# A six-layer megakernel on one core: weight loads, statistics and normalizations ahead of its mLSTM layer in another order

## The chip, the cores and the metric

The kernel runs on one core of one Trainium2 chip. One launch computes all six layers. The metric is the device time of the launch in microseconds (us), the median of several runs.

## The reference

The input x has 32 batches of 256 tokens with 128 channels, all float32. Six blocks are added to x one after another: an expert-choice feed-forward ("choice"), an RWKV attention, the first feed-forward again, a top-2 mixture of experts ("top2"), an mLSTM attention, and the top2 mixture again. Each block first normalizes x over its channels, without a gain.

```python
x = x + 0.5 * _L0_ffn_ref(_layernorm(x), ...)        # choice
x = x + _L0_attn_ref(_layernorm(x), ...)             # rwkv
x = x + 0.5 * _L0_ffn_ref(_layernorm(x), ...)        # choice
x = x + 0.5 * _L1_ffn_ref(_layernorm(x), ...)        # top2
x = x + _L1_attn_ref(_layernorm(x), ...)             # mlstm
x = x + 0.5 * _L1_ffn_ref(_layernorm(x), ...)        # top2
# mlstm, NH = 4 heads of DH = 32:
q, k, v, o = x @ Wq, x @ Wk, x @ Wv, x @ Wo
ig = 15 * tanh((x @ Wig + big) / 15); fg = 15 * tanh((x @ Wfg + bfg) / 15)
log_D[i, j] = cumsum(log_sigmoid(fg))[i] - cumsum(...)[j] + ig[j]   for j <= i
m = max_j log_D; D = exp(log_D - m); C = (q @ k.T) / sqrt(DH) * D
h = C @ v / (max(|C.sum(-1)|, exp(-m)) + 1e-6)
out = (sigmoid(o) * multi_head_norm(h)) @ Wdown
```

The gates ig and fg need every token of every batch before the cumulated sums are taken, so in the kernel all 32 batches pass through the gate product before the first step of the attention itself.

## The kernel before, in words

X, the whole activation, lives in SBUF as 64 tiles of 128 tokens by 128 channels; a batch is two tiles. The program is written engine by engine with explicit semaphores, and each engine runs its instructions in the order in which the code writes them. Six layers follow each other; between most of them the work overlaps batch by batch. The first top2 layer is different: its blocks write their rows to a table in DRAM (rt_y) by token number, so X can be loaded back only when all blocks have been sent. This is where the change lies.

At the end of the first top2 layer, SyncE (SP) waits for all sends and then issues eight loads of X, each of a "piece" of FB = 4 batches (`Top2.sync`, L894 to L896). VectorE (DVE), at the end of `Top2.vector` (L827 to L829), waits for each piece, adds 4 to the semaphore x_done and calls `Moments.moments_loaded` (L236): eight bn_stats, one a tile (`spread`, L266), and eight bn_aggr (`gather`, L272). GpSimd (POOL) makes from these the negative mean and the reciprocal deviation of the piece in three instructions on 128 by 8 numbers (`Moments.rstd`, L284, L285, L295) and counts them in the semaphore "scaled". The statistics have two buffers, so a piece's statistics wait until the piece two before has been scaled.

Then the mLSTM layer begins. SP, TensorE (PE), ScalarE (ACT) and DVE wait in `Shared.start` until x_done has counted all 32 batches. SP issues seven loads of weights and biases (`Mlstm.sync`, L1769 to L1771). DVE waits for them (L2105), sets a column of ones, scales Wdown by the head norm's weights (L2106, L2107), and normalizes batch after batch (`Normed.vector`, L332: two instructions, one a tile, into two alternating buffers mlstm_xn; batch b waits until the transposes of batch b-2 have read the buffer). For each batch PE makes two transposes into a PSUM bank (`turn_first`, L1792) and, after ACT has copied them to SBUF as mlstm_xT (L1899), two narrow products with the gate weights (`score`, L1801). When all 32 batches are scored, DVE does the gate math (`gate_math`, from L1989), PE transposes the gates, DVE takes the cumulated sums (`row_math`), and at the end of that chain the attention's steps start. The PE also waits, before its first transpose, for the scaled Wdown.

The same form of work stands once more in the program, at its very start: the first choice layer takes statistics of the loaded pieces and, behind each piece, normalizes the four batches of the piece before (`moments_first` with `between`).

The three lines that name the order in the first layer:

```python
            self.take(dve, FB * c, FB, FB * c, slice(0, FB * TP), c % 2)
            if between is not None and c:
                between(c - 1)
```

Of the kernel before, what the change touches and what calls it, by code (L numbers as in the profile page):

```python
# [24 lines left out]
B, T, C = 32, 256, 128  # L25
TP = T // P
# [16 lines left out]
FB = 4  # L43
# [149 lines left out]
class Moments:  # L193
# [39 lines left out]
        if layer < len(LAYERS) and inside(b):  # L233
            self.rstd(pool, layer, b, 1, b, slice(0, TP), u)

    def moments_loaded(self, dve, layer, c):  # L236
        n = layer * B + FB * c
        if c == 0:
            dve.wait_ge(self.scaled, n)
        self.take(dve, n, FB, FB * c, slice(0, FB * TP), c % 2)  # L240

    def scale_loaded(self, pool, layer, c):
        self.rstd(pool, layer, c, FB, FB * c, slice(0, FB * TP), c % 2)
# [134 lines left out]
class Top2(Layer):  # L378
# [392 lines left out]

    def vector(self, dve):
        sh, w = self.sh, self.w
        m = sh.moments
        for r, part in self.ORDER[2:]:
            (self.choose if part == "choose" else self.page)(dve, r)
        if not self.run:
# [43 lines left out]
        xlo(0, 0)  # L821
        xlo(0, 1)
        self.blocks(dve, step, 0, self.NBLK + 2)

        if self.run:
            return
        for c in range(XC):  # L827
            dve.wait_ge(sh.x_loaded[c], 32).then_inc(sh.x_done, FB)
            m.moments_loaded(dve, self.layer + 1, c)  # L829


    def centring(self, pool):
# [38 lines left out]
    def sync(self, sp):  # L871
        d = self.dispatch
        self.w.split.once(sp, self.w.sync)
        self.w.split.ready(sp)
        sp.wait_ge(self.sent, 16 * NT * (self.run + 1))

        def load(i, u):
            m = u % self.RING
            v, n = self.ring(i, u, -self.RING, self.YR)
            if self.block(i, u, -self.RING) or self.run:  # L880
                need(sp, self.y_sent[v], 16 * n)
            sp.dma_start(self.xs[:, m, :], d.region[self.run][bass.ds(P * (self.RING * i + u), P), :]).then_inc(self.xs_in[m], 16)

        def step(i, u):
            if self.block(i, u):
                load(i, u)

        self.blocks(sp, step, 0, self.NBLK - 1)
        for m in range(self.YR):
            sp.wait_ge(self.y_sent[m], 16 * self.turns(m, self.YR) * (self.run + 1))  # L890
        if self.run:
            return
        rows = d.y[self.run].rearrange("(p n) c -> p n c", p=P)
        for c in range(XC):  # L894
            part = slice(c * NT // XC, (c + 1) * NT // XC)
            sp.dma_start(self.sh.X[:, part, :], rows[:, part, :]).then_inc(self.sh.x_loaded[c], 16)  # L896


class Top2Weights:
# [791 lines left out]
class Mlstm(Layer):  # L1691
# [70 lines left out]
            step(s, s % 2)  # L1762

    LOADS = ("ml_wq", "ml_wk", "ml_wvo", "ml_wdown", "ml_wgate", "ml_norm_w")

    def sync(self, sp):
        a = self.sh.args
        self.sh.start(sp, self.x0)
        for dst, n in zip((self.wq, self.wk, self.wvo, self.wd0, self.wgate, self.nw), self.LOADS):  # L1769
            sp.dma_start(dst[:, :], a[n]).then_inc(self.w_in, 16)  # L1770
        sp.dma_start(self.bias[:, :], a["ml_bias"].to_broadcast([P, 2 * NH])).then_inc(self.w_in, 16)  # L1771
        sp.wait_ge(self.rows, 4)
        dst = self.run_dram.rearrange("b (h t) -> (b h) t", h=NH)
        sp.dma_start(dst, self.r_negrun[:, :]).then_inc(self.run_stored, 16)
        sp.wait_ge(self.run_stored, 16)
        sp.wait_ge(self.cols_done, 1)

        def row(b, u):
            need(sp, self.d_done, b - 1)
            dst = self.run_row[:, u, :, :].rearrange("p h t -> p (h t)")  # L1780
            sp.dma_start(dst, self.run_dram[bass.ds(b, 1), :].to_broadcast([P, NH * T])).then_inc(self.row_in[u], 16)

        pipeline(sp, row, 0, B - 1, 2, B - 3)

    def tensor(self, pe):
# [95 lines left out]
            if B <= s < B + 3:  # L1881
                self.after.scores(pe, 8 * (s - B), 8 * (s - B) + 8)

        sh.start(pe, self.x0)
        pe.wait_ge(sh.consts, sh.N_CONSTS)
        pe.wait_ge(self.setup, 1 + Rwkv.SETUP)
        turn_first(0, 0)
        for b in range(B):
            score(b, b % 2)
        turn_gates()  # L1890
        pe.wait_ge(self.cols_done, 1)
        project_qk(0)
        project_vo(0)
# [2 lines left out]
    def scalar(self, act):  # L1896
# [58 lines left out]
            if s == B + 1:  # L1955
                self.after.gate_exp(act, 0)

        self.sh.start(act, self.x0)
        for b in range(B):
            xT(b, b % 2)  # L1960
        act.wait_ge(self.gates, 1)
# [14 lines left out]
    def vector(self, dve):  # L1976
# [123 lines left out]
            if s == B + 2:  # L2100
                self.after.page(dve, 0)

        sh.start(dve, self.x0)
        dve.wait_ge(sh.consts, sh.N_CONSTS)
        dve.wait_ge(self.w_in, 16 * (len(self.LOADS) + 1 + Rwkv.LOADED))  # L2105
        dve.memset(self.ones[:, :], 1.0)  # L2106
        dve.tensor_scalar(self.wd[:, :], self.wd0[:, :], self.nw[:, 0:1], 0.5, ALU.mult, ALU.mult).then_inc(self.setup, 1)  # L2107
        for b in range(B):
            self.norm.vector(dve, b, b % 2, lambda: apart(dve, self.xT_ready, b - 1, sh.passed))
        gate_math()  # L2110
        row_math()
        self.steps(step)
# [92 lines left out]
def build(nc, args, out):  # L2205

    with ExitStack() as ctx:  # L2207
# [37 lines left out]
        def stand(n):  # L2245

            layer, place, run = layers[n]
            if LAYERS[n] == "rwkv" and n + 1 < len(layers) and LAYERS[n + 1] == "choice":
                layer.next = layers[n + 1][0]
                layer.next.stand(*layers[n + 1][1:])  # L2250
            layer.stand(place, run)
            if LAYERS[n] in ("choice", "mlstm"):
                layer.after = layers[n + 1][0] if LAYERS[n + 1] == "top2" else None
                if layer.after is not None:
                    layer.after.stand(*layers[n + 1][1:])
            return layer
# [88 lines left out]
```

## Time and profile before

| | us |
|---|---|
| median of 3 runs | 1860.92 |
| lowest, highest | 1853.59, 1864.89 |
| the profiled execution, its own time | 1842.0 |
| its span, first to last instruction | 1840.0 |
| mean granted TensorE clock, as a share of full speed | 0.881 |
| busy in the span: PE, DVE, ACT, POOL | 1470.1, 1357.5, 1020.1, 1106.3 |

All times in the rows are us from the start of the span. The profiled execution's time is 2.0 us above its span, and 18.9 us under the median of the timed runs. A row of the timeline gives the start, the length, the engine, the line, the operation with its output and inputs, the count of instructions merged in it, and in brackets how long the engine had been idle before it and what ended that. SPq is the queue of DMA issues of SyncE. The stretch in question lies between 1190 and 1260 us.

### The profile page before, as it was taken

Reading aid. Unit: us, or ns where it says so; the run is one execution under the profiler, and the core shown is the slowest. Engines: PE = TensorE matmul, PEld = TensorE weight load, DVE = VectorE, ACT = ScalarE, POOL = GpSimd, SP = SyncE. Lnnn points to the kernel's source line nnn. Section 1 sums busy time; section 2 is a strip of 40 time slices with the busy share of each in tenths; the row PEclk is TensorE's granted clock in tenths of the full one; section 3 lists DMA queues with packets and bytes.
Section 4 is the critical chain, followed back from the end, with each engine's and each line's share of the span. In section 5 each row is a group of like instructions: output and inputs, shape, how many; then the busy total and the mean of one; then the engine's idle time right before and its main releaser. Section 6 shows DMA issues by size and latency. Waiting matters only on the chain. (4 is left out here: it accounts for less than half of the span.)

```text
span 1840.0 us, 39778 instructions
## 1 busy us (share of the span) xinstructions
PE 1470.1 (80%) x10450; PEld 1350.9 (73%) x10450; DVE 1357.5 (74%) x4037; ACT 1020.1 (55%) x2524; POOL 1106.3 (60%) x1749
## 2 busy tenths in 40 slices
PE   6399999767772999999635999746999986069996
PEld 6289999756662899998514999745888875059996
DVE  7759899769996588888763777564677856447775
ACT  2288888623330888887113666513777741046764
POOL 4527787768882345543474666630598864746665
PEclk9999999979995999999667999855898976579998
DMA  5010100092000111000312222131222200122210
GB/s 183 27 44 30 35 31 24 1 221 61 0 0 19 47 36 33 31 24 2 120 51 60 65 64 55 25 89 38 82 89 73 93 1 27 55 61 64 65 52 13
DMA packets 93269, 96.18 MB, mean 52 GB/s; under 512 B 12073, under 2 KB 75710, under 8 KB 92577
## 3 DMA queue, kind: packets, MB, share of 16 engines
q1 hardware_dynamic: 83168, 76.70, 14.3%
q0 software_dynamic: 9920, 17.35, 2.8%
q8 instruction: 80, 1.31, 0.3%
q14 instruction: 101, 0.82, 0.1%
HBM read 63.75 MB, written 33.78 MB: 53 GB/s over the span
## 5 line engine op out<-in xcount | busy, mean ns | idle before, releaser
L1343 DVE TENSOR_TENSOR choice_hlo<-choice_h,choice_hhi 128x512 fp32r<-128x512 f32 x256 | 172.5, 715 | 47.0 <-ACT choice_hhi L1218 46.1
L1210 ACT ACTIVATE choice_h<-banks 128x512 f32<-128x512 f32 x256 | 152.2, 600 | 60.0 <-PE banks L1122 45.8
L795 DVE SCALAR_TENSOR_TENSOR top_h<-top_silu,top_xs,banks 128x176 f32<-128x176 f32 x364 | 128.6, 395 | 56.2 <-ACT top_silu L639 56.2
L844 POOL DMA_INDIRECT rt_rows<-X,top_slot x128 | 128.3, 1002 | 38.8 <-issue 38.8
L1120 PE MATMUL banks<-choice_xin_hi,ec_w_hi 128*128 128x256 f32 x512 | 145.7, 285 | 6.2 <-ACT choice_xin_lo L1203 4.7
L639 ACT ACTIVATE top_silu<-banks,top_xs 128x352 f32<-128x352 f32 x182 | 100.8, 554 | 88.1 <-PE banks L563 88.1
L1133 PE MATMUL banks<-choice_hhi,ec_w_hi 128*128 128x256 f32 x512 | 145.9, 285 | 3.1 <-DVE choice_hlo L1343 3.1
L1218 ACT ACTIVATE choice_hhi<-choice_h 128x512 fp32r<-128x512 f32 x256 | 146.6, 625 | 0.0
L1122 PE MATMUL banks<-choice_xin_hi,ec_w_lo 128*128 128x256 f32 x512 | 143.9, 281 | 0.0
L1121 PE MATMUL banks<-choice_xin_lo,ec_w_hi 128*128 128x256 f32 x512 | 143.8, 281 | 0.0
L1135 PE MATMUL banks<-choice_hhi,ec_w_lo 128*128 128x256 f32 x512 | 143.2, 280 | 0.0
L1134 PE MATMUL banks<-choice_hlo,ec_w_hi 128*128 128x256 f32 x512 | 143.1, 279 | 0.0
L850 POOL TENSOR_TENSOR top_y<-top_y,top_xs 128x128 f32<-128x128 f32 x182 | 82.3, 452 | 88.0 <-DVE top_y L809 87.2
L561 PE MATMUL banks<-t_w,top_xhi 128*128 x364 | 135.1, 371 | 0.0
L1429 POOL TENSOR_SCALAR choice_y_hi_lo<-choice_yw 128x512 fp32r<-128x512 f32 x64 | 41.5, 649 | 153.8 <-ACT choice_yw L1233 152.6
L581 PE MATMUL banks<-t_w,top_hhi 128*128 x364 | 129.7, 356 | 1.7 <-DVE top_y L809 1.6
L801 DVE TENSOR_TENSOR top_hlo<-banks,top_hhi 128x384 fp32r<-128x384 f32 x182 | 101.5, 558 | 37.6 <-ACT top_hhi L644 32.9
L562 PE MATMUL banks<-t_w,top_xhi 128*128 x364 | 119.1, 327 | 0.0
L563 PE MATMUL banks<-t_w,top_xlo 128*128 x364 | 118.9, 327 | 0.0
L543 PE MATMUL banks<-ident,top_xs 128*128 128x128 f32 x182 | 50.6, 278 | 81.2 <-issue 45.8
L857 POOL DMA_INDIRECT out_x<-top_y,top_xs x91 | 90.8, 997 | 34.5 <-issue 30.9
L857 POOL DMA_INDIRECT rt_y<-top_y,top_xs x91 | 90.3, 992 | 32.2 <-issue 29.7
(305 smaller groups left out, 5478.6 us busy)
## 6 DMA issues: line engine op xcount, KB each, us to landing
choice_token_row<-choice_tokens SPq DMA_DIRECT2D x64, 256.0 KB, 3.1
mlstm_run_row<-mlstm_run SPq DMA_DIRECT2D x32, 512.0 KB, 3.6
rt_rows<-rt_blank SPq DMA_DIRECT2D x2, 6188.0 KB, 35.9
top_xs<-rt_rows SPq DMA_DIRECT2D x182, 68.0 KB, 1.9
X<-in_x SPq DMA_DIRECT2D x8, 512.0 KB, 6.5
ec_stage<-in_ec_w SPq DMA_DIRECT2D x2, 2048.0 KB, 11.6
X<-rt_y SPq DMA_DIRECT2D x8, 512.0 KB, 7.0
rt_rows<-X,top_slot POOLq DMA_INDIRECT x128, 2.3
```

The lines of the kernel that those rows point to most:

```text
L561: pe.matmul(out, hi, w_hi, start=True, stop=False)
L581: pe.matmul(out[:, 0:2 * C], self.hhi[:, u % 4, k], tile[:, bass.ds(at, 2 * C)], start=(n == 0), stop=False)
L857: pool.indirect_dma_start(d.y[self.run], bass.IndirectOffsetOnAxis(ap=at, axis=0), y, None, bounds_check=NT * P - 1, oob_is_err=False).the ...
L1120: pe.matmul(o, w.w1_hi[:, e, k], hi, start=True, stop=False)
L1121: pe.matmul(o, w.w1_hi[:, e, k], lo, start=False, stop=False)
L1122: i = pe.matmul(o, w.w1_lo[:, e, k], hi, start=False, stop=True)
L1133: pe.matmul(o, w.w2_hi[:, e, c, :], self.hhi[:, ue, c, :], start=(c == 0), stop=False)
L1134: pe.matmul(o, w.w2_hi[:, e, c, :], self.hlo[:, ue, c, :], start=False, stop=False)
L1135: i = pe.matmul(o, w.w2_lo[:, e, c, :], self.hhi[:, ue, c, :], start=False, stop=(c == HC - 1))
L1210: act.activation(self.h[:, c, :], self.ph[c][:, :], ACT.Gelu).then_inc(self.gelu_done, 1)
L1218: act.activation(o, self.h[:, c, :], ACT.Copy).then_inc(self.hhi_done, 1)
L1343: dve.tensor_tensor(flat(self.hlo), self.h[:, c, :], flat(self.hhi).bitcast(F32), ALU.subtract).then_inc(self.hlo_done, 1)
```

## The change

It does four things. The seven loads of the mLSTM weights are issued behind the first piece of X, inside `Top2.sync`, by a new function `Mlstm.load_weights`. DVE's statistics of the loaded pieces move from the end of the top2 layer into the mLSTM layer, and `moments_loaded` takes a function `between`: before the two bn_stats of the k-th batch of piece c, batch 4(c-1)+k-2 is normalized; the last six batches are normalized behind the loop. The waits of SP, PE, ACT and DVE for the whole of X at the head of the layer go; the DVE's wait for the weights, its column of ones and the scaling of Wdown stand behind all normalizations. PE's wait for the scaled Wdown moves behind the gate transposes, and it waits for the gate weights ahead of its first product.

```diff
--- before.py
+++ after.py
@@ -233,11 +233,19 @@
         if layer < len(LAYERS) and inside(b):
             self.rstd(pool, layer, b, 1, b, slice(0, TP), u)
 
-    def moments_loaded(self, dve, layer, c):
+    def moments_loaded(self, dve, layer, c, between):
+
         n = layer * B + FB * c
         if c == 0:
             dve.wait_ge(self.scaled, n)
-        self.take(dve, n, FB, FB * c, slice(0, FB * TP), c % 2)
+        dve.wait_ge(self.sh.x_loaded[c], 32).then_inc(self.sh.x_done, FB)
+        apart(dve, self.scaled, n - FB, self.sh.passed)
+        for k in range(FB):
+            between(FB * (c - 1) + k - 2)
+            for t in range(TP * k, TP * k + TP):
+                i = dve.bn_stats(self.st[:, c % 2, t, :], self.sh.X[:, TP * FB * c + t, :])
+        i.then_inc(self.stats, FB)
+        self.gather(dve, n, FB, slice(0, FB * TP), c % 2)
 
     def scale_loaded(self, pool, layer, c):
         self.rstd(pool, layer, c, FB, FB * c, slice(0, FB * TP), c % 2)
@@ -771,7 +779,6 @@
 
     def vector(self, dve):
         sh, w = self.sh, self.w
-        m = sh.moments
         for r, part in self.ORDER[2:]:
             (self.choose if part == "choose" else self.page)(dve, r)
         if not self.run:
@@ -822,12 +829,6 @@
         xlo(0, 1)
         self.blocks(dve, step, 0, self.NBLK + 2)
 
-        if self.run:
-            return
-        for c in range(XC):
-            dve.wait_ge(sh.x_loaded[c], 32).then_inc(sh.x_done, FB)
-            m.moments_loaded(dve, self.layer + 1, c)
-
 
     def centring(self, pool):
         if not self.run:
@@ -894,6 +895,8 @@
         for c in range(XC):
             part = slice(c * NT // XC, (c + 1) * NT // XC)
             sp.dma_start(self.sh.X[:, part, :], rows[:, part, :]).then_inc(self.sh.x_loaded[c], 16)
+            if c == 0:
+                self.follow.load_weights(sp)
 
 
 class Top2Weights:
@@ -1762,13 +1765,16 @@
             step(s, s % 2)
 
     LOADS = ("ml_wq", "ml_wk", "ml_wvo", "ml_wdown", "ml_wgate", "ml_norm_w")
-
-    def sync(self, sp):
+    WEIGHTS_IN = 16 * (len(LOADS) + 1 + Rwkv.LOADED)
+
+    def load_weights(self, sp):
+
         a = self.sh.args
-        self.sh.start(sp, self.x0)
         for dst, n in zip((self.wq, self.wk, self.wvo, self.wd0, self.wgate, self.nw), self.LOADS):
             sp.dma_start(dst[:, :], a[n]).then_inc(self.w_in, 16)
         sp.dma_start(self.bias[:, :], a["ml_bias"].to_broadcast([P, 2 * NH])).then_inc(self.w_in, 16)
+
+    def sync(self, sp):
         sp.wait_ge(self.rows, 4)
         dst = self.run_dram.rearrange("b (h t) -> (b h) t", h=NH)
         sp.dma_start(dst, self.r_negrun[:, :]).then_inc(self.run_stored, 16)
@@ -1881,13 +1887,13 @@
             if B <= s < B + 3:
                 self.after.scores(pe, 8 * (s - B), 8 * (s - B) + 8)
 
-        sh.start(pe, self.x0)
         pe.wait_ge(sh.consts, sh.N_CONSTS)
-        pe.wait_ge(self.setup, 1 + Rwkv.SETUP)
         turn_first(0, 0)
+        pe.wait_ge(self.w_in, self.WEIGHTS_IN)
         for b in range(B):
             score(b, b % 2)
         turn_gates()
+        pe.wait_ge(self.setup, 1 + Rwkv.SETUP)
         pe.wait_ge(self.cols_done, 1)
         project_qk(0)
         project_vo(0)
@@ -1955,7 +1961,6 @@
             if s == B + 1:
                 self.after.gate_exp(act, 0)
 
-        self.sh.start(act, self.x0)
         for b in range(B):
             xT(b, b % 2)
         act.wait_ge(self.gates, 1)
@@ -2100,13 +2105,18 @@
             if s == B + 2:
                 self.after.page(dve, 0)
 
-        sh.start(dve, self.x0)
+        def normalize(b):
+            if inside(b):
+                self.norm.vector(dve, b, b % 2, lambda: apart(dve, self.xT_ready, b - 1, sh.passed))
+
         dve.wait_ge(sh.consts, sh.N_CONSTS)
-        dve.wait_ge(self.w_in, 16 * (len(self.LOADS) + 1 + Rwkv.LOADED))
+        for c in range(XC):
+            sh.moments.moments_loaded(dve, self.layer, c, normalize)
+        for b in range(B - FB - 2, B):
+            normalize(b)
+        dve.wait_ge(self.w_in, self.WEIGHTS_IN)
         dve.memset(self.ones[:, :], 1.0)
         dve.tensor_scalar(self.wd[:, :], self.wd0[:, :], self.nw[:, 0:1], 0.5, ALU.mult, ALU.mult).then_inc(self.setup, 1)
-        for b in range(B):
-            self.norm.vector(dve, b, b % 2, lambda: apart(dve, self.xT_ready, b - 1, sh.passed))
         gate_math()
         row_math()
         self.steps(step)
@@ -2249,6 +2259,8 @@
                 layer.next = layers[n + 1][0]
                 layer.next.stand(*layers[n + 1][1:])
             layer.stand(place, run)
+            if LAYERS[n] == "top2":
+                layer.follow = layers[n + 1][0] if n + 1 < len(layers) else None
             if LAYERS[n] in ("choice", "mlstm"):
                 layer.after = layers[n + 1][0] if LAYERS[n + 1] == "top2" else None
                 if layer.after is not None:
```

On DVE, between the last block of the first top2 layer and the gate math, the program of before stands as follows (the first two rows are there eight times, once a piece).

```order
L266 BN_STATS bnstats<-X 128x6 x8
L272 BN_AGGR moments<-bnstats 128x2 x8
...
L2106 MEMSET mlstm_ones 128x1
L2107 TENSOR_SCALAR mlstm_wdown<-mlstm_wdown_in,mlstm_norm_w 128x128
L332 TENSOR_SCALAR mlstm_xn<-X,negmean,rstd 128x128 x64
L1989 TENSOR_TENSOR mlstm_g_raw<-banks,mlstm_gate_bias 128x512
```

On DVE at the same place, the changed program has this; here are the pieces 0, 1 and 2 and the end (L246 and L340 are the same statistics and normalizations, under new line numbers).

```order
L246 BN_STATS bnstats<-X 128x6 x8
L280 BN_AGGR moments<-bnstats 128x2 x8
L246 BN_STATS bnstats<-X 128x6 x4
L340 TENSOR_SCALAR mlstm_xn<-X,negmean,rstd 128x128 x2
L246 BN_STATS bnstats<-X 128x6 x2
L340 TENSOR_SCALAR mlstm_xn<-X,negmean,rstd 128x128 x2
L246 BN_STATS bnstats<-X 128x6 x2
L280 BN_AGGR moments<-bnstats 128x2 x8
...
L340 TENSOR_SCALAR mlstm_xn<-X,negmean,rstd 128x128 x12
L2118 MEMSET mlstm_ones 128x1
L2119 TENSOR_SCALAR mlstm_wdown<-mlstm_wdown_in,mlstm_norm_w 128x128
```

From piece 2 on, a normalization of one batch (two instructions) stands ahead of every two statistics, four batches a piece; six batches are left for the end, and the ones and Wdown stand behind them.

On SP, at the end of the first top2 layer, the program of before issues this.

```order
L896 DMA X<-rt_y 128x8x128 x8
L1770 DMA mlstm_wq<-in_ml_wq 128x128
L1770 DMA mlstm_wk<-in_ml_wk 128x128
L1770 DMA mlstm_wvo<-in_ml_wvo 128x256
L1770 DMA mlstm_wdown_in<-in_ml_wdown 128x128
L1770 DMA mlstm_wgate<-in_ml_wgate 128x8
L1770 DMA mlstm_norm_w<-in_ml_norm_w 128x1
L1771 DMA mlstm_gate_bias<-in_ml_bias 128x8
```

On SP the changed program issues this.

```order
L897 DMA X<-rt_y 128x8x128
L1774 DMA mlstm_wq<-in_ml_wq 128x128
L1774 DMA mlstm_wk<-in_ml_wk 128x128
L1774 DMA mlstm_wvo<-in_ml_wvo 128x256
L1774 DMA mlstm_wdown_in<-in_ml_wdown 128x128
L1774 DMA mlstm_wgate<-in_ml_wgate 128x8
L1774 DMA mlstm_norm_w<-in_ml_norm_w 128x1
L1775 DMA mlstm_gate_bias<-in_ml_bias 128x8
L897 DMA X<-rt_y 128x8x128 x7
```

The seven small loads now stand ahead of seven of the eight pieces of X.

## Rows read from the trace of the kernel before

**Rows 1.** Waits between 1190 and 1278 us: in total, times, longest.

```profile
PE banks L1792 <- DVE mlstm_xn L332: 34.4, 1, 34.4
DVE mlstm_xn L332 <- PE banks L1792: 16.8, 29, 1.0
...
DVE mlstm_ones L2106 <- DMA mlstm_gate_bias<-in_ml_bias: 2.5, 1, 2.5
```

**Rows 2.** Timeline from the loads of X to the third piece's statistics.

```profile
1192.90 11.29 SPq L896 DMA_DIRECT2D X<-rt_y  x8
1197.64 1.64 DVE L266 BATCH_NORM_STATS2 bnstats<-X 128x6 f32<-128x128 f32 x8 [10.12 <-DMA X<-rt_y]
1199.43 0.64 DVE L272 BATCH_NORM_AGGREGATE moments<-bnstats 128x2 f32<-128x6 f32 x8
1199.99 1.61 DVE L266 BATCH_NORM_STATS2 bnstats<-X 128x6 f32<-128x128 f32 x8
1200.26 0.20 POOL L284 TENSOR_TENSOR negmean<-moments,minus_one 128x8 f32<-128x8 f32 x1 [8.60 <-DVE moments L272]
...
1200.88 1.67 POOL L295 TENSOR_TENSOR rstd<-rstd_steps,minus_half 128x8 f32<-128x8 f32 x1 [0.15 <-POOL rstd_steps L285]
...
1202.70 1.65 DVE L266 BATCH_NORM_STATS2 bnstats<-X 128x6 f32<-128x128 f32 x8 [0.31 <-POOL rstd L295]
```

**Rows 3.** Timeline at the head of the mLSTM layer.

```profile
1214.79 0.35 SPq L1770 DMA_DIRECT2D mlstm_wq<-in_ml_wq  x1
...
1217.55 0.43 SPq L1771 DMA_DIRECT2D mlstm_gate_bias<-in_ml_bias  x1
...
1220.47 1.11 DVE L332 TENSOR_SCALAR mlstm_xn<-X,negmean,rstd 128x128 f32<-128x128 f32 x4
...
1221.21 1.11 PE L1792 MATMUL banks<-ident,mlstm_xn 128*128 128x128 f32 x4 [34.43 <-DVE mlstm_xn L332]
```

**Rows 4.** Timeline of the last batches' normalizations, up to the gate math.

```profile
1254.61 0.60 DVE L332 TENSOR_SCALAR mlstm_xn<-X,negmean,rstd 128x128 f32<-128x128 f32 x2 [0.57 <-PE banks L1792]
...
1254.96 0.67 PE L1792 MATMUL banks<-ident,mlstm_xn 128*128 128x128 f32 x2
...
1256.14 0.67 PE L1792 MATMUL banks<-ident,mlstm_xn 128*128 128x128 f32 x2
...
1257.31 0.67 PE L1792 MATMUL banks<-ident,mlstm_xn 128*128 128x128 f32 x2
...
1259.52 0.69 DVE L1989 TENSOR_TENSOR mlstm_g_raw<-banks,mlstm_gate_bias 128x512 f32<-128x512 f32 x1 [3.13 <-PE banks L1801]
```

**Rows 5.** Stretches: busy time (instructions) by engine, granted clock, DMA share, rate.

```profile
core 0: us, PE busy (x) PEld busy (x) DVE busy (x) ACT busy (x) POOL busy (x), PEclk, DMA share, GB/s
1206.00:1208.00 2.00, 0.00 (x0) 0.00 (x0) 1.85 (x15) 0.00 (x0) 1.66 (x2) 0.50 1.19 304
1216.00:1218.00 2.00, 0.00 (x0) 0.00 (x0) 1.60 (x13) 0.00 (x0) 1.66 (x2) 0.50 0.56 148
1220.00:1258.00 38.00, 36.70 (x186) 36.17 (x187) 19.32 (x66) 11.89 (x31) 0.18 (x1) 0.50 0.00 1
1285.00:1320.00 35.00, 33.61 (x242) 29.88 (x243) 18.55 (x55) 25.26 (x77) 16.11 (x28) 0.78 0.26 91
```

**Rows 6.** Timeline of one piece in the first choice layer.

```profile
20.33 0.64 DVE L272 BATCH_NORM_AGGREGATE moments<-bnstats 128x2 f32<-128x6 f32 x8
20.89 1.08 DVE L332 TENSOR_SCALAR choice_xn<-X,negmean,rstd 128x128 f32<-128x128 f32 x4
21.15 0.20 POOL L284 TENSOR_TENSOR negmean<-moments,minus_one 128x8 f32<-128x8 f32 x1 [3.18 <-DVE moments L272]
...
21.77 1.70 POOL L295 TENSOR_TENSOR rstd<-rstd_steps,minus_half 128x8 f32<-128x8 f32 x1 [0.15 <-POOL rstd_steps L285]
...
24.05 1.64 DVE L266 BATCH_NORM_STATS2 bnstats<-X 128x6 f32<-128x128 f32 x8
...
25.83 0.64 DVE L272 BATCH_NORM_AGGREGATE moments<-bnstats 128x2 f32<-128x6 f32 x8
```

## The prediction

> **What bounds the kernel here.** I read the busy tenths of the page first; they show a hollow at about two thirds of the span. The waits of that stretch come next [rows 1]: PE waits once, for 34.4 us, for the first normalized batch, and afterwards DVE waits 29 times, 16.8 us in all, for PE's transposes. So two phases follow each other, one in which PE has nothing and one in which PE sets the pace. The timeline gives their edges. SP issues X's loads at 1192.90, the first piece is used at 1197.64 [rows 2], the first transpose starts at 1221.21 [rows 3], and the gate math starts at 1259.52 [rows 4]. Everything behind it (gate math, cumulated sums, the attention's steps, the last top2 layer) hangs on that start, because DVE's first gate instruction needs the products of all 32 batches. I take it that a shift of 1259.52 reaches the end of the program in full.
>
> In the second phase a transpose pair starts every 1.17 to 1.18 us [rows 4]; PE is busy for 36.70 of 38 us [rows 5]. 32 batches at 1.17 are 37.5 us. In the first phase DVE takes statistics: a piece costs 2.35 us (1197.64 to 1199.99) where nothing holds it [rows 2].
>
> **The change, part by part.** *The statistics between the normalizations.* DVE's own work for a piece of four batches is 2.35 us for the statistics and 4 x 0.54 for the normalizations (four instructions, two batches, take 1.08 [rows 6]): 4.51 us. PE needs 4 x 1.17 = 4.69 for the same four batches. The sum of work would thus just fit PE's pace. What does not fit is the order. In piece c the third normalization is of the first batch of piece c-1, and needs POOL's result for it. Count from the start A of piece c-1's aggregation. The next statistics or normalization can start at A+0.56 (1199.43 to 1199.99 [rows 2]). Then stand two normalizations (1.08) and four statistics (half of 1.64, 0.82), so DVE reaches the third normalization at A+2.46. POOL's result reaches DVE at A+3.27: the aggregation starts at 1199.43, and the third piece's statistics, held by POOL, start at 1202.70 [rows 2]. Beside normalizations POOL's power instruction takes 1.70 where it took 1.67 [rows 2, 6], so A+3.30. DVE stands still for 3.30 - 2.46 = 0.84 us in each piece, and a piece takes 4.51 + 0.84 = 5.35 us. The bounds: not below PE's 4.69, and on the other side the first choice layer, which does the same work with the statistics in one lump, needs 5.50 (20.33 to 25.83 [rows 6]). I take 5.35, near the upper row and explained by its own count.
>
> Now the sum. Piece 0 is as before: aggregation at 1199.43. Batch 0 can be normalized at 1202.70, the very time at which POOL's first result let DVE go before. Then one normalization, two statistics, one normalization, two statistics and 0.15 (1.79 from statistics to aggregation less their 1.64 [rows 2]): 1202.70 + 0.54 + 0.41 + 0.54 + 0.41 + 0.15 = 1204.75 for piece 1's aggregation. Six more pieces: 1204.75 + 6 x 5.35 = 1236.85. The last piece's first batch, number 28, can be normalized 3.30 later, at 1240.15. Its transposes follow 0.74 later (1220.47 to 1221.21 [rows 3]), at 1240.89; PE is free by then, since batches 26 and 27 came to it at about 1238.2 and 1239.4. Three more batches at 1.17: 1244.40. From the last transposes to the gate math it is 1259.52 - 1257.31 = 2.21 [rows 4]: 1246.6. Before, it was 1259.52. **The gain is 12.9 us.**
>
> *The weights behind X's first piece.* Before, DVE waited 2.5 us for the last of them [rows 1]; that is contained in the 12.9. What it costs is X's second piece. The seven issues take 1217.55 + 0.43 - 1214.79 = 3.2 us on SP [rows 3], and every later piece is issued that much later at worst. The second piece was there by 1199.99 at the latest [rows 2]; so it is there by 1203.2 at the latest. Counted from its own issue, about 1196.5, with the 4.7 us that the first took (1192.90 to 1197.64 [rows 2]), it is there at 1201.2. The weights' own traffic is small: 0.56 of 2 us of the DMA engines [rows 5]. DVE needs four statistics (0.82) before batch 0's normalization at 1202.70, so a piece that is there by 1201.9 costs nothing. I take 0, with bounds of 0 and 1.3 us. The later pieces are due every 5.35 us and come every 1.7 (0.52 MB at 304 GB/s [rows 5]).
>
> *The waits for the whole of X* on PE, ACT, SP and DVE: nothing by themselves, since each of these engines then waits for something that comes later (the first normalized batch, its transposes, the gate row). What stood behind SP's wait were only the weights.
>
> *Ones and Wdown behind the normalizations.* About 0.3 us of DVE, at about 1243, while DVE would wait until 1246.6 for PE; hidden by 3 us. PE's wait for Wdown stands behind the gate transposes, over 10 us later. PE's new wait for the gate weights ahead of its first product, at about 1204.6: they were issued by 1196.5 and landed long before.
>
> **A rule weighed.** Now POOL's three instructions are on the path, and normalizations stand beside them. In the first choice layer POOL's chain from aggregation to power instruction has four normalization instructions beside it, and starts at the same distance, 0.82 to 0.83 us, with 1.70 in place of 1.67 for the long one [rows 2, 6]. The Trainium skill's page "SBUF — State Buffer", section "Who interferes with whom", says that a VectorE instruction in a two-port mode (a float32 tensor_scalar from SBUF can be one) and a GpSimd instruction exclude each other for their whole length. By that rule POOL would lose up to the normalizations' time; by the row it loses 0.03. I keep the row.
>
> **The rivals.**
> 1. *POOL held off by the normalizations.* For it: in the new order the two normalizations are spread out, one from A+0.56 and one from A+1.51, so the second meets the start of the power instruction, which no row shows. Against: [rows 6]. Price: POOL later by at most the second normalization and half of the first, 0.8 us a piece, seven times: 5.6 us. The gain falls to 7.3: 1853.6. The page named above would give this case.
> 2. *X late.* The second piece at 1203.2 or later, 1.3 us lost: 1849.3. For it: it queues behind small-row loads; against: the 4.7 us from issue to use.
> 3. *PE sets the pace.* If POOL's result does not hold DVE (it would have to come by A+2.6), a piece costs 4.69: 4.0 us more gain, 1844.0. Against it are the 3.27 us of [rows 2]. Even PE busy without a gap from 1203.4 (1202.70 + 0.74) ends at 1203.4 + 31 x 1.17 + 2.21 = 1241.9, a gain of 17.6. By mechanism alone a gain over 1% (18.6 us) is out of reach.
> 4. *The change doesn't do what it says:* the first normalization comes early but DVE keeps alternating between waits for POOL and for PE, and only the 2.5 us of weights are won: 1858.4. Against: 4.51 of DVE's work fit in PE's 4.69.
> 5. *Slower, by the clock.* PE's granted clock is 0.50, the lower level of 1.2 GHz, through the whole pass although PE is busy for 36.70 of 38 us, and it is 0.78 on the mean in the first steps of the attention [rows 5]. If the earlier start met the clock's return so that those steps ran at 0.50, the 33.61 us of PE there would become 33.61 x 0.78 / 0.50 = 52.4, 18.8 us more; less the 12.9, it is 5.9 slower: 1866.8. It decides from two thirds of that stretch on (12.9 of 18.8). Against: from 1259.52 on every instruction stands as before, so what PE does before the rise stays the same.
>
> **How the numbers follow.** The sum against the profiled execution: 1842.0 - 12.9 = 1829.1. The shown median is 18.9 above that execution; I carry the difference over: 1860.9 - 12.9 = 1848.0. Chances: forecast 0.66, rival 1 0.10, rival 2 0.08, rival 3 0.07, rival 4 0.05, rival 5 0.04. The runs of before lie from 1853.6 to 1864.9, so a median may be off by 4 or 5 us by itself; with the bounds of the pace (1844.0 to 1853.6) this gives a range from 1838 to 1859. One per cent is about what a measurement of this kernel tells from no change. The forecast of 0.7% lies within it; the scatter lifts some of the forecast and of rival 3 over the edge: faster 0.13, within 1% 0.82, slower 0.05 (rival 5 and scatter).
>
> **What would show it.** In the profile after: PE's first wait in this stretch ends near 1203.4 instead of 1221.21; statistics and normalizations alternate on DVE, with aggregations 5.35 us apart, and one wait of about 0.8 us a piece for POOL's rstd; PE waits a little in each piece for mlstm_xn; DVE's wait for the bias load is gone; the gate math starts near 1246.6. Rival 1 would show in L295 above 1.75 us or its start beyond 1.5 us from the aggregation's start; rival 2 in a wait of DVE for X at the second piece; rival 3 in aggregations 4.7 us apart; rival 5 in the clock of the first attention steps. The forecast is wrong if the gate math starts where I say and the end of the span moves by less than 10 or more than 16 us, or if the pass itself does not shrink.

## The result, and the profile after

The changed kernel took 1845.86 us in the median of its runs, the kernel before 1857.12 us in the same comparison: a ratio of 0.9946, with a 95% interval from 0.9925 to 0.9966, that is 10.0 us less (6.3 to 13.9). Forecast were 1848.0 and 12.9 us less. The change is 0.5%, within the one per cent that I had called the edge. One of the changed kernel's 16 runs took 2935.88 us, at a granted clock of 1.00 where the others have 0.87 to 0.88; it counts in the median (1844.89 without it) but not in the ratio, and what happened in it is not known.

The profiled execution of the changed kernel lasted 1855.18 us, 13 more than the profiled one of before. Two single executions thus say nothing about the change; the stretches in them do. I use a local clock: from SP's first issue of X to the start of the gate math. Before it is 1259.52 - 1192.90 = 66.6 us [rows 2, 4]. These are the rows of the changed kernel's timeline that answer to them (L246, L280, L303, L340 and L1798 are before's L266, L272, L295, L332 and L1792).

```profile
1203.20 0.37 SPq L897 DMA_DIRECT2D X<-rt_y  x1
1203.62 0.57 SPq L1774 DMA_DIRECT2D mlstm_wq<-in_ml_wq  x1
...
1207.09 9.50 SPq L897 DMA_DIRECT2D X<-rt_y  x7
1207.50 1.65 DVE L246 BATCH_NORM_STATS2 bnstats<-X 128x6 f32<-128x128 f32 x8 [10.24 <-DMA X<-rt_y]
...
1211.68 0.87 DVE L246 BATCH_NORM_STATS2 bnstats<-X 128x6 f32<-128x128 f32 x4 [1.75 <-DMA X<-rt_y]
1212.57 0.60 DVE L340 TENSOR_SCALAR mlstm_xn<-X,negmean,rstd 128x128 f32<-128x128 f32 x2
...
1213.32 0.66 PE L1798 MATMUL banks<-ident,mlstm_xn 128*128 128x128 f32 x2 [16.79 <-DVE mlstm_xn L340]
...
1225.51 0.64 DVE L280 BATCH_NORM_AGGREGATE moments<-bnstats 128x2 f32<-128x6 f32 x8
...
1226.19 0.60 DVE L340 TENSOR_SCALAR mlstm_xn<-X,negmean,rstd 128x128 f32<-128x128 f32 x2
1226.33 0.26 POOL L292 TENSOR_TENSOR negmean<-moments,minus_one 128x8 f32<-128x8 f32 x1 [3.12 <-DVE moments L280]
...
1226.85 0.69 PE L1798 MATMUL banks<-ident,mlstm_xn 128*128 128x128 f32 x2 [0.20 <-DVE mlstm_xn L340]
...
1227.01 1.64 POOL L303 TENSOR_TENSOR rstd<-rstd_steps,minus_half 128x8 f32<-128x8 f32 x1 [0.15 <-POOL rstd_steps L293]
...
1228.04 0.67 PE L1798 MATMUL banks<-ident,mlstm_xn 128*128 128x128 f32 x2
...
1228.91 0.60 DVE L340 TENSOR_SCALAR mlstm_xn<-X,negmean,rstd 128x128 f32<-128x128 f32 x2 [0.82 <-PE banks L1798]
...
1230.95 0.64 DVE L280 BATCH_NORM_AGGREGATE moments<-bnstats 128x2 f32<-128x6 f32 x8
...
1257.08 0.69 DVE L1994 TENSOR_TENSOR mlstm_g_raw<-banks,mlstm_gate_bias 128x512 f32<-128x512 f32 x1 [2.93 <-PE banks L1807]
```

The first transpose starts 10.1 us after X's first issue, where before it was 28.3. Aggregations are 5.44 us apart (1225.51 to 1230.95), and once in each such interval DVE stands still for 0.82 or 0.83 us (in one of them for 0.39 and 0.46, at two places). The gate math starts 53.9 us after X's first issue: the stretch is 12.7 us shorter, 12.9 were forecast. Some 0.4 us of the 12.7 are chance: in the profile of before, X's first piece was used 4.74 us after its issue, and in the other eleven executions of this study, of before too, after 4.15 to 4.51. In the waits of the stretch these lines answer to those of before [rows 1]; the wait for the bias load is gone, and the normalizations wait for PE 7 times instead of 29.

```profile
PE banks L1798 <- DVE mlstm_xn L340: 20.2, 14, 16.8
...
DVE bnstats L246 <- DMA X<-rt_y: 12.0, 2, 10.2
...
DVE mlstm_xn L340 <- PE banks L1798: 5.1, 7, 0.8
...
DVE mlstm_xn L340 <- POOL rstd L303: 2.2, 2, 1.8
```

One thing in these rows speaks against my explanation. Of the 7 waits, 5.1 us, that are put down to PE's transposes, five are the 0.8 us waits in question, where I had said that POOL's rstd holds DVE; only in one interval does the row name POOL, for 0.46 us. In the timeline the transposes of the batch before end at 1228.71 and POOL's rstd at 1228.65, 0.06 us apart, so the times cannot decide it. The program's order can: batch b waits only for the transposes of batch b-2, which used the same buffer. The normalization at 1228.91 is that of batch 12. The transposes that end at 1228.71 are batch 11's, which it does not need; batch 10's are those of 1226.85, and they ended at 1227.54, 1.4 us before DVE went on. So the name in the wait row is wrong here. Two experiments show the same without that count.

The clock rows show no rival 5. PE was at 0.50 through the pass as before [rows 5]; the first line here is the pass of the changed kernel, the second the first steps of its attention, at 0.80 where before had 0.78.

```profile
1213.00:1256.00 43.00, 39.20 (x188) 37.64 (x188) 32.24 (x173) 12.29 (x32) 14.68 (x21) 0.50 0.22 56
...
1283.00:1318.00 35.00, 34.17 (x249) 30.92 (x250) 21.52 (x58) 24.95 (x75) 15.93 (x27) 0.80 0.28 93
```

### The profile page after: what moved, and what is told of

The parts are those of the page before. It is cut to its first block, busy times and chain, and to the rows that moved or that the text cites. A ratio compares the mean times of both kernels' runs of the same rounds, so it can differ in the third digit from the quotient of the medians.

```text
span 1853.2 us, 39778 instructions
## 1 busy us (share of the span) xinstructions
PE 1478.7 (80%) x10450; PEld 1359.7 (73%) x10450; DVE 1359.3 (73%) x4037; ACT 1021.3 (55%) x2524; POOL 1107.9 (60%) x1749
## 4 chain that ended last, share of the span: by engine, by line
PE 57%; DVE 16%; issue 11%; POOL 9%; ACT 3%; DMA 2%; another core or an unknown queue 2%; DVEq 0%; SPq 0%; POOLq 0%; ACTq 0%
PE banks L589 5%; PE banks L578 3%; PE banks L569 3%; PE banks L1136 3%; PE banks L570 3%; PE banks L571 3%; PE banks L1123 3%; PE banks L1125 3%; PE banks L1124 3%; PE banks L1158 3%; PE banks L1138 3%; PE banks L1137 3%; POOL rt_rows L845 2%; PE banks L590 2%; PE banks L1108 2%
## 5 line engine op out<-in xcount | busy, mean ns | idle before, releaser
L303 POOL TENSOR_TENSOR rstd<-rstd_steps,minus_half 128x2 f32<-128x2 f32 (+2 forms) x112 | 99.1, 885 | 13.9 <-POOL rstd_steps L293 9.2
```

## The experiments

Theory 1 is the forecast's: once a piece DVE waits for POOL's rstd, and nothing else stands between it and PE's pace. Theory 2 is what the wait rows name: PE's transposes hold DVE.

**Every normalization one batch later** (label e1_later). The piece's first batch now comes as the fourth, not the third.

```diff
-            between(FB * (c - 1) + k - 2)
+            between(FB * (c - 1) + k - 3)
...
-        for b in range(B - FB - 2, B):
+        for b in range(B - FB - 3, B):
```

> The changed kernel, with every normalization one batch later: batch 4(c-1)+k-3 ahead of the k-th statistics pair of piece c, seven batches left for the end. The clock of this study is local: from SP's first issue of X to the start of the gate math. It was 66.6 us before (1192.90 to 1259.52) and 53.9 after (1203.20 to 1257.08). Theory 1, POOL's rstd holds DVE once a piece (by 0.83 us): now the piece's first batch is reached about 3.4 us behind the aggregation's start, when POOL has just finished, so aggregations stand 4.7 us apart in place of 5.44, PE sets the pace, and the local time is 49.6 us; the kernel is 4 us faster than the changed one, 15 to 17 faster than before. Theory 2, PE's transposes hold DVE there, as the wait row names them: the distance stays 5.44, the local time 53.9 to 54.3, the whole 11 us faster than before.

Measured: a local time of 49.9 us (1193.41 to 1243.29), and a ratio to before of 0.9922 (0.990 to 0.9945), 14.4 us less. DVE's timeline of two aggregations, between them POOL's result and the normalization that needs it:

```profile
1218.26 0.64 DVE L280 BATCH_NORM_AGGREGATE moments<-bnstats 128x2 f32<-128x6 f32 x8
...
1219.76 1.64 POOL L303 TENSOR_TENSOR rstd<-rstd_steps,minus_half 128x8 f32<-128x8 f32 x1 [0.15 <-POOL rstd_steps L293]
...
1221.81 0.60 DVE L340 TENSOR_SCALAR mlstm_xn<-X,negmean,rstd 128x128 f32<-128x128 f32 x2
...
1222.95 0.64 DVE L280 BATCH_NORM_AGGREGATE moments<-bnstats 128x2 f32<-128x6 f32 x8
...
1243.29 0.69 DVE L1994 TENSOR_TENSOR mlstm_g_raw<-banks,mlstm_gate_bias 128x512 f32<-128x512 f32 x1 [2.93 <-PE banks L1807]
```

The interval is 4.69, which is PE's 4 x 1.17, and from 1213 to 1240 us PE has no idle time:

```profile
1213.00:1240.00 27.00, 27.00 (x139) 26.93 (x139) 22.65 (x121) 8.81 (x23) 10.49 (x15) 0.50 0.01 2
```

Had PE's transposes been what held DVE, a later place for the same normalization could not have shortened the interval. With the count above, theory 2 falls.

**One more power instruction on GpSimd** (label e5_pool_longer), the opposite test.

```diff
         else:
+            if count == FB:
+                pool.tensor_tensor(sm[:, 1, :], sm[:, 0, :], half, ALU.pow)
             i = pool.tensor_tensor(flat(self.rs), sm[:, 0, :], half, ALU.pow)
```

> The changed kernel with one more power instruction of 1.65 us on GpSimd in each loaded piece, ahead of the one that gives rstd; its result is not used. It stands in the first layer too, outside the local stretch. Theory 1 (DVE waits for rstd once a piece, PE only seems to hold it): each of the seven intervals, and the first normalization, gets 1.65 to 1.7 us longer: aggregations 7.1 us apart, local time 53.9 + 13.4 = 67.3 us. Theory 2 (PE's transposes hold DVE): 0.83 us of POOL's extra time is hidden behind them or the distance does not change: local time 54 to 60 us.

Measured: intervals of 6.97 us (1207.77 to 1214.74, and on), 1.53 more than 5.44, and a local time of 66.1 us (1194.9 to 1261.04), 12.2 more. The instruction costs 1.53 us an interval and not 1.65 to 1.7: the two power instructions start 1.60 us apart (1209.20 and 1210.80), and the first of them starts 0.28 us after the step ahead of it, where it was 0.35 (1226.66 to 1227.01). The wait carries POOL's name now, as the longer chain has moved away from PE's transposes:

```profile
1210.80 1.64 POOL L305 TENSOR_TENSOR rstd<-rstd_steps,minus_half 128x8 f32<-128x8 f32 x1
1212.70 0.60 DVE L342 TENSOR_SCALAR mlstm_xn<-X,negmean,rstd 128x128 f32<-128x128 f32 x2 [2.36 <-POOL rstd L305]
```

From the aggregation to POOL's end it was 3.14 us (1225.51 to 1228.65) and is 4.67 (1207.77 to 1212.44), 1.53 more; the wait grew from 0.83 to 2.36 us, by the same 1.53, so nothing of the extra time was hidden. POOL's result had been the last thing to come before, too. With the run above this shows theory 1.

**Only the weight loads moved** (label e3_loads_only), the kernel before otherwise.

```diff
             sp.dma_start(self.sh.X[:, part, :], rows[:, part, :]).then_inc(self.sh.x_loaded[c], 16)
+            if c == 0:
+                self.follow.load_weights(sp)
...
-        self.sh.start(sp, self.x0)
```

> The kernel before, with only the seven weight loads moved behind X's first piece; statistics of all pieces first, waits for the whole of X kept. Theory 1 (the interleaving carries the gain): DVE's wait of 2.5 us for the bias load goes, its second piece comes 1.4 us later, and a wait of 0.3 for POOL goes: local time 66.6 - 2.5 + 1.4 - 0.3 = 65.2 us. Rival (the loads' place carries a larger part): below 63 us.

Measured: 65.5 us (1192.24 to 1257.71). Of the 12.7 us the loads' place alone brings 1.1, or 0.7 against the second profile of before (66.2, below); the interleaving, with the waits for the whole of X gone, brings the rest. The price of the loads is seen at the second piece, 8.8 us after X's first issue instead of 7.1 (1199.99 - 1192.90 [rows 2]):

```profile
1201.06 1.64 DVE L266 BATCH_NORM_STATS2 bnstats<-X 128x6 f32<-128x128 f32 x8 [2.08 <-DMA X<-rt_y]
...
1218.66 1.11 DVE L332 TENSOR_SCALAR mlstm_xn<-X,negmean,rstd 128x128 f32<-128x128 f32 x4
```

**The weight loads behind X's last piece** (label e2_weights_last), the changed kernel otherwise.

```diff
-            if c == 0:
+            if c == XC - 1:
                 self.follow.load_weights(sp)
```

> The changed kernel, with the seven weight loads issued behind the last piece of X instead of the first. If the weights' place is free (they only have to be there for the end), the local time from X's first issue to the gate math stays 53.9 us. If PE's first product, which needs the gate weights, is the point: the loads are issued about 11.3 us after X's first issue and landed at about 17, PE stands until then (its first product was at 11.5), DVE fills its two buffers and stands in batch 4 from 14.8 to about 18.6, and since DVE sets the pace afterwards nothing of that is caught up: 57.5 us. The second piece of X comes about 1.4 us earlier, which gains nothing, because the first normalization waits for POOL until 9.4 to 9.8 us.

Measured: 59.2 us (1198.25 to 1257.49), 5.3 more than the changed kernel and 1.7 more than expected. The direction was right; the place where it stops was one batch earlier than I had read in the code. PE's wait for the weights stands ahead of the second batch's transposes, which belong to the first `score`, so DVE stands at the fourth normalization already, and PE's wait is one of 6.94 us:

```profile
1216.17 0.69 PE L1798 MATMUL banks<-ident,mlstm_xn 128*128 128x128 f32 x2 [6.94 <-DMA mlstm_gate_bias<-in_ml_bias]
...
1217.01 0.60 DVE L340 TENSOR_SCALAR mlstm_xn<-X,negmean,rstd 128x128 f32<-128x128 f32 x2 [5.47 <-PE banks L1798]
```

So the interleaving needs the early loads: alone they bring 0.7 to 1.1 us, under it they are worth 5.3. The start of this run's pass is needed below: POOL's first rstd, and the first normalization.

```profile
1206.00 1.67 POOL L303 TENSOR_TENSOR rstd<-rstd_steps,minus_half 128x8 f32<-128x8 f32 x1 [0.15 <-POOL rstd_steps L293]
...
1207.82 0.60 DVE L340 TENSOR_SCALAR mlstm_xn<-X,negmean,rstd 128x128 f32<-128x128 f32 x2 [1.88 <-POOL rstd L303]
```

**Statistics in a lump** (label e4_lump), four normalizations behind the eight statistics of the next piece.

```diff
-        for k in range(FB):
-            between(FB * (c - 1) + k - 2)
-            for t in range(TP * k, TP * k + TP):
-                i = dve.bn_stats(self.st[:, c % 2, t, :], self.sh.X[:, TP * FB * c + t, :])
+        for t in range(FB * TP):
+            i = dve.bn_stats(self.st[:, c % 2, t, :], self.sh.X[:, TP * FB * c + t, :])
         i.then_inc(self.stats, FB)
         self.gather(dve, n, FB, slice(0, FB * TP), c % 2)
+        for k in range(FB):
+            between(FB * (c - 1) + k)
```

> The changed kernel, but with the statistics of a piece in one lump and behind them the four normalizations of the piece before, as in the first choice layer; four batches are left for the end. If any overlap of the two passes does it, and the fine alternation adds little: a piece every 5.50 us as in the first choice layer, first normalization at about 10.8 us, local time 55.0 us against 53.9. If the fine alternation is what hides the statistics: a piece at 4.0 or more above PE's 4.69, that is 6 us or more, and a local time over 58 us.

Measured: 54.4 us (1192.8 to 1247.18), an interval of 5.50. The fine alternation of the changed kernel is worth only 0.5 us over the coarse order, because what it saves in waits for PE (0.38 and 0.57 us a piece here) it gives to the wait for POOL (0.83). The aggregation row of this kernel, the two waits, and one interval on:

```profile
1208.05 0.64 DVE L280 BATCH_NORM_AGGREGATE moments<-bnstats 128x2 f32<-128x6 f32 x8
...
1210.07 0.60 DVE L340 TENSOR_SCALAR mlstm_xn<-X,negmean,rstd 128x128 f32<-128x128 f32 x2 [0.38 <-PE banks L1798]
...
1211.25 0.60 DVE L340 TENSOR_SCALAR mlstm_xn<-X,negmean,rstd 128x128 f32<-128x128 f32 x2 [0.57 <-PE banks L1798]
...
1213.55 0.64 DVE L280 BATCH_NORM_AGGREGATE moments<-bnstats 128x2 f32<-128x6 f32 x8
```

**Batches 0 to 3 early, the rest one batch later** (label e6_early_start).

```diff
-            between(FB * (c - 1) + k - 2)
+            at = FB * (c - 1) + k
+            if at < FB + 2:
+                between(at - 2)
+            elif at > FB + 2:
+                between(at - 3)
```

> The order of the run with every normalization one batch later, but batches 0 to 3 as early as in the changed kernel (two in piece 1, two at the head of piece 2). Theory 1 with PE's pace of 1.17 us as the floor: the first transpose starts about 0.4 us earlier, one small gap is left before batch 4, local time 49.3 us against 49.9. If PE is no floor, the local time falls below 48 us.

Measured: 50.1 us (1194.2 to 1244.33), not 49.3. PE begins 0.6 us earlier (9.3 against 9.9 us for the first normalization) and then has four gaps of 0.23, 0.42, 0.21 and 0.48 us before it runs at its pace, where the run with later normalizations has one of 1.05; I had counted one here too. The floor is PE's pace, and this order does not reach it sooner. The expected gain was a miss; the floor of 48 us was not broken.

**The changed kernel and the kernel before once more** (labels e8_after_again, e7_before_again).

> The changed kernel once more, with its own rounds beside the kernel before. Theory 1: the gain is the 12.7 us by which the stretch from X's first issue to the gate math became shorter, and nothing of it is lost or won behind it: local time 53.9 us again, 11 to 14 us faster than before; from the gate math to the last top2 layer's first store the profile shows 380 to 385 us, as before (381.8), since the 397.3 of the first profile of the changed kernel were waits of DVE without a local releaser, which are scatter. Rival: the change itself costs something behind the gate math: 390 us or more there again, and 5 us or less of gain.

> The kernel before once more, for a second profile. Local time 66.6 us; from the gate math to the last layer's first store 380 to 385 us if that stretch is as steady as the first profile says; if it shows 390 or more here, such waits come without the change too.

Measured: local times of 53.9 and 66.2 us; ratio of the changed kernel to before 0.9942 (0.9923 to 0.9961), 10.7 us less. From the gate math to the last layer's first store it is 378.4 us in the changed kernel and 380.4 in the one before.

**The changed kernel and the later normalizations side by side** (labels e9_after_beside, e10_later_beside).

> The changed kernel, timed on the same chip and in the same rounds as the kernel with the later normalizations. Theory 1: local time 53.9 us, 10 to 13 us faster than before.

> The kernel with every normalization one batch later, beside the changed one. Theory 1: local time 49.9 us, and the kernel's time is 4 us below the changed kernel's in the same rounds. Rival: the 4 us are given back behind the gate math, and the two times are within 1 us of each other.

Measured, in the same rounds: before 1859.37, changed 1846.40 (ratio 0.993, 0.9905 to 0.9955), later normalizations 1842.80 (ratio 0.9907, 0.9882 to 0.9933). Local times 53.9 and 49.7. The 3.6 us between the two medians are the 4.2 of the local clock within the scatter. That the later place saves 4 us is shown for the stretch, by the local clock, twice. That the kernel as a whole gains them is likely and not shown: two comparisons with before point that way (14.4 and 17.3 us by their ratios, against 10.0, 10.7 and 13.0), but the intervals of the two kernels overlap.

Where the total scatters is seen when the profiled executions are cut into stretches (us):

| execution | X's first issue at | local | gate math to first store | last layer's stores |
|---|---|---|---|---|
| before, first | 1192.9 | 66.6 | 381.8 | 190.0 |
| before, again | 1195.1 | 66.2 | 380.4 | 190.1 |
| later normalizations, first | 1193.4 | 49.9 | 379.4 | 189.9 |
| changed, again | 1194.3 | 53.9 | 378.4 | 190.0 |
| changed, first | 1203.2 | 53.9 | 397.3 | 190.1 |
| changed, beside | 1201.2 | 53.9 | 391.9 | 190.0 |
| later, beside | 1204.0 | 49.7 | 396.0 | 190.0 |

The five other experiments' profiles lie with the first four: X's first issue at 1192.2 to 1198.3, and 379.3 to 382.4 us behind the gate math. The last three executions of the table carry 3 to 12 us more ahead of X's issue than these nine, and 10 to 19 more behind the gate math. Only they have waits of DVE and ACT in the top2 layers' routing that no event on this core ends; the profile puts them down as "remote". Two lines, of the first profile of the changed kernel:

```profile
DVE top_n L755 <- remote: 18.8, 3, 10.2
...
DVE top_per_token L736 <- remote: 9.0, 1, 9.0
```

The changed kernel stands on both sides of this divide with the same instructions, so its instructions alone do not bring the waits. Nor do the waits need the change, it seems: the kernel before was at 1842.2 and 1842.58 us in the comparisons whose profiles lack these waits, and at 1857.12 and 1859.37 in those whose profiles have them. No profile of before fell into such a time, so for it this is inferred from times. What causes them stays open.

## Why the prediction was right

*The bound, and that a shift of the gate math reaches the end:* right, as far as the runs can tell. From the gate math to the last layer's first store, the nine executions without the waits in the routing take 378.4 to 382.4 us: 380.4 and 381.8 before, 378.4 in the changed kernel. So nothing over 4 us is won or lost there. Three comparisons of the whole kernel give 10.0, 10.7 and 13.0 us where the local clock gives 12.7, or 12.3 against the second profile of before; their intervals all hold both. I had named less than 10 us at the end as a sign of being wrong. The first comparison stands on that edge (6.3 to 13.9), the other two above it (7.2 to 14.2 and 8.4 to 17.7), and none of the intervals excludes less than 10. That the gain arrives in full is read from the stretches; the totals agree with it and do not prove it.

*The interval of 5.35 us, from 4.51 of DVE's work and 0.84 of waiting for POOL:* measured 5.44, and the wait 0.83. One term was too small, the start of a normalization behind POOL. I took 0.15 (1202.55 to 1202.70 in the timeline of before, from 1200.88 + 1.67 [rows 2]); in the steady pass a normalization starts 0.26 after POOL's end (1228.65 to 1228.91). By the program a second wait, for the buffer, stands there behind the one for POOL, while ahead of the statistics POOL's was the last. The first two batches have no buffer to wait for, and they come sooner: batch 0 starts 0.15 after POOL's end (1207.67 to 1207.82 in the run with the weights last). Behind the aggregation it is the same. The changed kernel's normalization starts 0.68 us after the aggregation's start (1225.51 to 1226.19), where I took 0.56; in the run with later normalizations it is 0.57 for batch 1 (1204.42 to 1204.99) and 0.68 for batch 5 (1208.96 to 1209.64). That fits the second wait as the cause, at about 0.11 us; no run takes it away by itself. So DVE's work is 4.61 us a piece, 5.44 less 0.83, and not 4.51. The wait came out right because both its ends moved by about as much, and that is luck.

*The start:* the first normalization was forecast 9.8 us after X's first issue and came at 9.37, since the first piece was there after 4.30 us instead of 4.74. My one profile of before had an unusually late piece, so this was luck too: it gave back 0.43 of the 0.64 us that the six intervals (0.09 each) and the last piece's start (0.10) lost. The second piece was used at 8.48 us: between my 8.3 (4.7 from its own issue) and the edge of 9.0 from which it would cost. The seven issues ahead of it took 3.5 us (1203.57 to 1207.09) and not 3.2. The later piece cost nothing that can be seen: from the aggregation to the first normalization it is 3.28 us (1209.29 to 1212.57), and 3.27 in the run with the weights last (1204.55 to 1207.82), where the second piece was there early.

*The end:* forecast 53.7 (1246.6 - 1192.9), measured 53.9, with the two errors above against each other.

*POOL held off by the normalizations (rival 1):* refuted here. POOL's first instruction takes 0.26 us in this order where it took 0.20, the power instruction 1.64, and the aggregation-to-POOL distance stays 0.82. The normalization does not lose either: one batch takes 0.59 us beside the power instruction (from 1227.10) and 0.59 with POOL idle (from 1224.38). The rule of the Trainium skill's page "SBUF — State Buffer" on the shared port pair (section "Who interferes with whom") would block POOL for the normalization's length where this runs in a two-port mode; nothing over 0.06 us is seen. So either the mode is not entered by a 128 by 128 float32 instruction with two per-partition scalars or the blocks do not meet. The runs don't tell which.

*X late (rival 2)* came in part and was hidden. *PE's pace (rival 3)* was no limit in the changed kernel; the run with later normalizations made it one, at 4.69 and 4 us of gain, just what rival 3's price said. *Only 2.5 us won (rival 4)* is refuted by the local clock. *The clock (rival 5)* did not show, but its sign was a weak one. From 25.5 to 60.5 us behind the start of the gate math the granted clock is 0.76 to 0.95 in the twelve executions, with 0.78 and 0.95 in the two of before, so it differs that much without any change. Its price was too high as well. By the working of rival 5 the step from 0.95 to 0.78 should cost 6.0 us there (33.61 - 33.61 x 0.78 / 0.95), and everything behind the gate math took 1.4 us longer at 0.78 than at 0.95 (381.8 and 380.4).

*The median:* 1848.0 against 1845.86. That it is so near is in part luck. The kernel before had 1857.12 in this comparison and not 1860.92, which alone is 3.8 us less, and the gain between the medians was 11.3 us and not 12.9, which is 1.6 more. That I carried 18.9 us from the profiled execution to the median worked for a reason that I did not know: the shown runs of before came, it seems, from a time with the waits in the routing, its profile from one without, and the comparison fell in such a time again.

## What to carry to other kernels

When two passes over the same data follow each other on one engine, and the second is paced by another engine, put the first between the steps of the second; then count, from the producer's start to the consumer's place in the order, whether the helper's result (here 3.4 us from the start of the aggregation, for eight numbers a partition) is there when the engine comes to it, and move the consumer back by one step if it is not. That step was worth a third of what the whole interleaving brought, for two digits in the code. And where two releasers end within 0.1 us of each other, the name in a wait row is no evidence: count in the program which instruction the semaphore asks for, then shift the one or lengthen the other.

## What was not expected of the hardware

PE's pace in this pass does not hang on its clock. The same order of statistics and normalizations took 5.50 us a piece in the first layer (20.33 to 25.83 [rows 6]), at a granted clock of 1.00 (2.4 GHz), and 5.50 us in the run with the statistics in a lump, at 0.50 (1.2 GHz). In both, DVE waits 0.38 and 0.57 us a piece for PE's transposes, two transposes take 0.67 us and four of the narrow products 0.86. The first line is the stretch in the first layer of before, the second the one around the lump's interval.

```profile
20.00:25.00 5.00, 4.36 (x24) 4.27 (x23) 3.90 (x22) 1.48 (x4) 2.10 (x3) 1.00 1.03 439
```

```profile
1208.00:1214.00 6.00, 5.69 (x30) 5.59 (x28) 4.85 (x31) 1.92 (x5) 2.09 (x3) 0.50 0.50 128
```

In the run with later normalizations PE was busy for 27.00 us of 27.00, in transposes and products of 8 columns, and the granted clock was 0.50 all through.
